# Graph attention in one kernel: one pair of look-ups a step, half a group further ahead, and the comparison lines a group sooner

## What is computed

```python
e = jax.nn.leaky_relu(a_s[src] + a_d[dst], NEG_SLOPE)
m = jax.ops.segment_max(e, dst, num_segments=n)
ex = jnp.exp(e - m[dst])
denom = jax.ops.segment_sum(ex, dst, num_segments=n)
alpha = ex / denom[dst]
msg = h[src] * alpha[:, :, None]
out = jax.ops.segment_sum(msg, dst, num_segments=n)
```

## Time and profile before

| | |
|---|---|
| median of 3 runs | 4394.04 us (4389.03 to 4397.5) |
| profiled execution, span | 4836.3 us |
| busy: PE, PEld, DVE, ACT, POOL | 3107.3, 1876.3, 3044.1, 2574.7, 2895.1 us |
| granted TensorE clock, mean | 0.796 |
| edge pass 1, edge pass 2 (roughly) | 1850 to 3224 us, 3364 to 4744 us |

### The profile page before, as it was taken

The page is one execution under the profiler, slowest core; times in us unless marked ns, Lnnn a source line. Parts: engine busy times, 40 slices in busy tenths (PEclk is TensorE's granted clock), DMA queues, the critical chain, the costliest instruction groups (busy, mean ns, idle before and its releaser), DMA issues. The chain is left out here.

```text
span 4836.3 us, 56702 instructions
## 1 busy us (share of the span) xinstructions
PE 3107.3 (64%) x11125; PEld 1876.3 (39%) x11125; DVE 3044.1 (63%) x8069; ACT 2574.7 (53%) x7729; POOL 2895.1 (60%) x2918
## 2 busy tenths in 40 slices
PE   4699999989998883455555555555354555555451
PEld 3344444444444372333333334433233333333331
DVE  7788888878887753455555455566354555555557
ACT  3598888888888642333334334344243334343347
POOL 2366666656665405677777767733676777777763
PEclk8899999999999996677777767778576777767776
DMA  5233323333322244444444444424444444444445
GB/s 165 93 88 87 86 86 86 87 85 86 87 85 84 72 127 134 112 129 118 129 123 124 129 118 129 131 61 127 117 126 121 122 125 128 118 129 124 124 108 161
DMA packets 274567, 540.54 MB, mean 112 GB/s; under 512 B 73156, under 2 KB 161983, under 8 KB 274240
## 3 DMA queue, kind: packets, MB, share of 16 engines
q0 software_dynamic: 134912, 376.36, 28.8%
q1 hardware_dynamic: 132308, 154.29, 10.3%
q10 hardware_dynamic: 7020, 6.40, 0.4%
HBM read 495.47 MB, written 41.31 MB: 111 GB/s over the span
## 5 line engine op out<-in xcount | busy, mean ns | idle before, releaser
L1247 POOL DMA_INDIRECT arena<-h_rows,idx x1856 | 1893.8, 1020 | 972.0 <-issue 515.2
L1382 PE MATMUL ps<-arena,z 128*128 128x264 f32 x3712 | 1328.7, 511 | 493.1 <-DVE arena L1494 290.8
L769 POOL DMA_INDIRECT arena<-y_rows,idx x928 | 901.0, 971 | 717.7 <-ACT arena L800 359.1
L1306 ACT ACTIVATE z<-z 128x256 f32<-128x256 f32 x928 | 382.2, 412 | 1504.0 <-remote 833.3
L1382 PEld LDWEIGHTS ps<-arena,z 128*128 128x128 f32 x3712 | 856.6, 249 | 728.2 <-DVE arena L1494 351.7
L1502 DVE TENSOR_TENSOR z<-ps,z 128x264 f32 x928 | 396.1, 427 | 1105.3 <-remote 713.3
L798 ACT ACTIVATE arena<-arena 128x128 f32<-128x128 f32 x2784 | 912.0, 393 | 110.8 <-DVE arena L885 64.4
L840 PE MATMUL ps<-arena 128*128 128x512 f32 x1856 | 902.5, 610 | 4.6 <-DVE z L893 4.6
L1298 ACT ACTIVATE z<-iota,dst_x 128x128 f32<-128x128 f32 x1856 | 644.5, 395 | 26.4
L1494 DVE TENSOR_TENSOR arena<-arena,z 128x520 f32<-128x520 f32 x928 | 639.0, 689 | 1.8 <-ACT z L1287 1.1
L832 PE MATMUL ps<-arena 128*128 128x512 f32 x928 | 495.6, 617 | 121.2 <-DVE arena L885 85.2
(11 more groups left out here) (231 smaller groups left out, 2838.3 us busy)
## 6 DMA issues: line engine op xcount, KB each, us to landing
z<-lo_rows SPq DMA_DIRECT2D x116, 512.0 KB
arena<-h_rows,idx POOLq DMA_INDIRECT x1856
arena<-y_rows,idx POOLq DMA_INDIRECT x928
z<-seg_rows SPq DMA_DIRECT2D x232, 64.0 KB
h_rows<-arena SPq DMA_DIRECT2D x98, 132.0 KB, 1.8
arena<-h_rows SPq DMA_DIRECT2D x98, 132.0 KB, 3.0
arena<-res_rows SPq DMA_DIRECT2D x98, 128.0 KB, 3.0
z<-in_ea_rows SPq DMA_DIRECT2D x464, 8.0 KB
```

Source lines behind the costliest of these rows:

```text
L769: pool.indirect_dma_start(out=ring[:, r, :], out_offset=None, in_=s.y_rows, in_offset=bass.IndirectOffsetOnAxis(ap=rows_of[:, u, n:n + 1], ...
L1247: pool.indirect_dma_start(out=ring[:, u * SCORED + n, :], out_offset=None, in_=h_rows, in_offset=bass.IndirectOffsetOnAxis(ap=s.idx[:, u, ...
L1306: nc.scalar.activation(sel[:, q % SELS, :, :].rearrange("p k n -> p (k n)"), away[:, q % 2, :, :].rearrange("p k n -> p (k n)"), ACT.Relu, ...
L1382: last = t.matmul(ps[:, bank[q % 4], 0:ROW], sel[:, q % SELS, k, :], ring[:, u * SCORED + 2 * q + k, :], start=(k == 0), stop=(k == 1))
```

## The change

Before, the 16 look-ups of group g+1 are issued two a step in steps 1 to 8 of group g, and the one-hot matrices that they need are written at steps 0 and 2 of the same group g. Afterwards TensorE issues one look-up in each step: in steps 0 to 7 of group g those of the second half of group g+1, in steps 8 to 15 those of the first half of group g+2. Eight more stand in front of the first group. VectorE writes the one-hot matrices of group g+2 at steps 2 and 10 of group g, and sums the first half at step 5 in place of step 7.

```diff
+    EARLY = STEPS_IN // 2
...
                     collect(g, u, q)
-                    if not final:
-                        if 0 <= q - 1 < STEPS_IN // 2:
-                            look_up(g + 1, 1 - u, 2 * (q - 1))
-                            look_up(g + 1, 1 - u, 2 * (q - 1) + 1)
+                    if q < EARLY and not final:
+                        look_up(g + 1, 1 - u, EARLY + q)
+                    if q >= EARLY and g + 2 <= last_group:
+                        look_up(g + 2, u, q - EARLY)
             for q in range(STEPS_IN):
                 look_up(0, 0, q)
+            for q in range(EARLY):
+                look_up(1, 1, q)
...
                         add(g, q - 1)
+                    if g + 2 <= last_group and q in (2, 10):
+                        one_hot(g + 2, 0 if q == 2 else 1)
                     if not final:
-                        n = {0: 0, 2: 1}.get(q)
-                        if n is not None:
-                            one_hot(g + 1, n)
-                        if q in (7, 10):
-                            own(g + 1, 0 if q == 7 else 1)
+                        if q in (5, 10):
+                            own(g + 1, 0 if q == 5 else 1)
...
             for i in range(2):
                 own(0, i)
+            for i in range(2):
+                one_hot(1, i)
```

## The result

| | median us | ratio to before |
|---|---|---|
| before | 4391.99 (4 runs, 4389.03 to 4397.5) | 1 |
| changed | 4415.43 (4 runs, 4411.05 to 4418.57) | 1.0053 (1.0039 to 1.0067) |

The change made the kernel slower by 0.53%, some 23 us. The forecast was 4389 us, with 4340 to 4415 us as the range; the measured time lies just above it, and the change went the other way than forecast. The execution that the rows ahead of the prediction come from was a disturbed one, 442 us above the timed runs, with late ("remote") semaphores that no later trace has; so a second trace of the kernel before (`n0_before_again`, span 4390.0 us) is set against the changed one from here on.

A forecast was written before the change was run, and what follows sets the result against it. The prediction took POOL's gathers to bound the edge passes (42.2 of 47.5 us a group); -1 us at the tail and -4 us from the comparison made -5 us, 4394 to 4389 us, range 4340 to 4415 us.

The forecast's parts named there:

- a tenth: Outside the edge passes: 2082 us assumed a tenth (208 us) shorter in timed runs, leaving the passes 234 us shorter.
- Its ceiling: Edge passes: POOL lost 211 us, 4.4% of the span, to waits for other engines, the most any gain could reach.
- Parts 1 to 6: Look-ups 0; comparison 0 to -37 us; TensorE's head stop 0 to -163; register load 0 to +42; waits 0; tail -1.
- 1, 3 and 4: Look-up count unchanged, 0; TensorE's 3.54 us head stop removed, 0 to -163 us; register load at step 8, 0 to +42 us.
- part 2: Comparison moves from VectorE's head path to step 10: 0 to -0.66 us a group, 56 times, 0 to -37 us.
- bounds of -163 us and +42 us: Largest gain from removing TensorE's head stop, with the comparison's 0.66 us; largest loss from the register load at step 8.
- The signs that the prediction named: Look-ups' comparison waits (105.2 us) near 0, `collect` of steps 2 and 3 sooner, `source` waiting for gathers over 8 times.
- The sum where POOL sets the pace: Whole kernel: -1 us, and -4 us for a tenth of the 37 us, giving -5 us, 4394 to 4389 us.
- one long gather beside the comparison: At a group's head: gather started at 2216.72, took 1.27 in place of 0.95 us, 0.72 us late in all.
- the lock-out at step 10: Rival: moved comparison locks out gathers at step 10, +40 us, 4434 us, if it formerly fell into POOL's wait; chance 0.06.
- The head counts: Rival: POOL waits for the ring in timed runs, partly through the head's stop; 4357 us, at most to 4231; chance 0.33.
- the register load at step 8: Rival: TensorE stops 0.75 us a group at step 8, in the catching-up half, +42 us, 4436 us; chance 0.12.

The follow-up runs named there:

- late_lookups: Kernel before with VectorE's order kept, comparisons for a group later, and all 16 look-ups and both register loads in steps 8 to 15: 4391.57 us, ratio 0.9998.
- psum_cmp_after: Changed kernel with `ex` in PSUM and the comparison as a tensor_tensor against a PSUM column: 4297.61 us, ratio 0.9784 to the kernel before.
- psum_cmp_before: Kernel before with `ex` in PSUM and the comparison as a tensor_tensor against a PSUM column: 4301.44 us, ratio 0.9792.

## Why the prediction was wrong

**What bounds the kernel.** Right in its core: POOL at its own pace in the timed runs, as argued from the 442 us, and now shown by 58 waits of `source`. The share of the 442 us that it put into the passes was an assumption ("a tenth") and came out near: from the first gather to the last of each pass, the two are 253 us shorter in the second trace, where it had 234. Its ceiling was wrong: of the 211 us that POOL was said to lose to the other engines nothing is left in the second trace. The real ceiling was the 99 us by which gathers took longer than 0.946 us.

**Parts 1 to 6.** Each was given 0 or nearly so in the forecast, and none shows: all that isn't gathers differs by 2.2 us between the two traces (2535.4 and 2533.2 us), within the 4 us by which that column varies anyway. late_lookups tests 1, 3 and 4 at once, with a ratio of 0.9998. The 4 us that the forecast took from part 2 were for groups in which POOL waits for the ring, and there are none. The bounds of -163 us and +42 us were both for paths that don't exist when POOL is the limit. The signs that the prediction named came: the comparison's waits nearly gone, `collect` of step 2 sooner, `source` waiting 58 times. They confirm the mechanism that it had, and say nothing of the one that it lacked.

**The step that failed** is the sum itself: "The sum where POOL sets the pace: -1 us, and -4 us". It counted what VectorE and TensorE do as free once POOL is the limit, and so left no term for how the moved comparison changes POOL's own instructions. That term comes to +21.1 us of gathers in the trace (+36 us from step 10 on, -15 us at the head); the timed runs are 23 us apart. The gathers' mean of 1.020 us over a median of 0.949 us said that 132 us of 1893.8 us were lost in them already; the prediction took the mean as fixed work, "work of POOL that the change doesn't touch". It did look at one long gather beside the comparison, and put what it found into a rival and not into the sum.

**The rival that came nearest** was the lock-out at step 10, with a chance of 0.06 and +40 us. It had POOL as the limit and a moved VectorE instruction that lengthens gathers. From step 10 on the loss was indeed 36 us. But the gather that the comparison itself overlaps there (gather 7) took only 4.5 us of it; 27.5 us are gather 8, held by the messages that the comparison pushed back. That its size came so near is luck. The rival also left out that without the comparison at step 0 everything behind it at the head lies sooner against the gathers, the comparison of step 2 included, which gave 15 us back. Its point of decision ("if the comparison used to fall into a wait of POOL") was wrong too, as was the prediction's sentence that the place makes no difference as long as a gather is always running: POOL has no such waits, the gathers follow each other 0.30 us apart, and what counts is which part of it the instruction falls on.

How much the comparisons cost can be counted in two ways. Gathers that run beside a comparison exceed 0.946 us by 39.7 us in sum before and by 18.9 us in the changed kernel, all others by 59 and 101 us; since a gather can have a comparison and a message beside it, this is no clean division. Taken out one after the other, moving `ex` shortens the gathers by 60.4 us (before) and 85.2 us (changed), moving the comparison's operand as well by another 30.1 and 31.9 us. The second pair is what comparisons cost once the messages are harmless and everything has shifted, and not their share in the two kernels compared here.

**The head counts** (0.33) and **the register load at step 8** (0.12) are both refuted. late_lookups takes TensorE's stop away and has both register loads in the catching-up half, at 0.9998; and the gathers' waits for the ring are the usual 0.30 us each.

**Two operands in SBUF.** The Trainium skill (SBUF — State Buffer, Who interferes with whom) also has a rule that the prediction passed over: a VectorE instruction with two SBUF inputs contends with a GpSimd instruction that reads SBUF. A gather here takes its row numbers from `idx` in SBUF, and the runs agree with the rule, by 60 and 85 us for one operand moved to PSUM. The same section says that `tensor_tensor` did not stall a DMA of GpSimd in a test, and gives as the inferred reason that descriptor generation needs only the write interface. For these indirect gathers a `tensor_tensor` does, by some 0.5 us; whether that is the reading of `idx` or the descriptors, no run here tells.

What stays open: which access of the gather is held up, since the traces show only that its end moves to near the end of the message; and why psum_cmp_after is ahead of psum_cmp_before by 5.5 us of gathers and 9.0 us of span (3.8 us in the timed runs).

## What to carry to other kernels

When GpSimd's indirect gathers set the pace, sort them by duration. Here every gather that took over 1.2 us (163 before, 214 in the changed kernel) had a `message`, which reads two operands from SBUF, or the bf16 comparison beside it. In this kernel the order of the other engines' work counted for nothing by itself, not even a real stall that was removed. Four reorderings and one neutral sum cost 0.5% to 0.9% through alignment alone, while a fifth reordering, which kept VectorE's order, cost nothing. So test such a change against a neutral pad before believing in its reason. The cure was not a better order but one operand in PSUM: for the multiplication it cost no time and gave 1.4 to 1.5%, and with the comparison's operand as well, at three times the comparison's time, 2.1 to 2.2%.

## What was not expected of the hardware

- A `message` of 128x520 f32 that starts just before the end of a gather of 0.95 us lengthens it to 1.42 to 1.47 us, until the message is nearly through. One that runs wholly within a gather costs it nothing (267 gathers of the changed kernel, 0.946 us in the mean).
- The hold-up works both ways: in the second trace of before the comparison at step 0, at 2016.85, took 0.94 us beside a gather; the one at step 2, at 2019.60, took 0.74 us and lengthened gather 17. Of 116 comparisons 50 took over 0.85 us there, and 1 in the changed kernel.

```profile
2016.85 0.94 DVE L1415 TENSOR_SCALAR z<-z,p_f 128x2048 bf16<-128x2048 bf16 x1
...
2019.60 0.74 DVE L1415 TENSOR_SCALAR z<-z,p_f 128x2048 bf16<-128x2048 bf16 x1
```

- The same multiplication takes 686 ns in the mean with one operand in PSUM and 687 ns with both in SBUF.
